# Layer 2's pass of a graph network: stored lookup one-hots loaded two batches at a time into four buffers

## What is computed

```
h = maximum(layernorm(x), 0)
message = h[src] * (edge_weight_n2 * edge_weight)[:, None]
x = x + segment_sum(message, dst, num_segments=6250)
```

## Time and profile before

| what | us |
|---|---|
| median of three runs | 7052.06 |
| the runs | 7048.93 to 7054.1 |
| span of the profiled execution | 7043.7 |
| layer 2's pass in it, first DMA issue to last accumulation (4152.3 to 4887.1) | 734.8 |

### The profile page before, as it was taken

The page is one execution under the profiler, slowest core; times in us unless marked ns, Lnnn a source line. Parts: engine busy times, 40 slices in busy tenths (PEclk is TensorE's granted clock), DMA queues, the critical chain, the costliest instruction groups (busy, mean ns, idle before and its releaser), DMA issues. The chain is left out here.

```text
span 7043.7 us, 136888 instructions
## 1 busy us (share of the span) xinstructions
PE 4278.3 (61%) x28588; PEld 2975.8 (42%) x28784; DVE 4223.4 (60%) x20793; ACT 3158.6 (45%) x10013; POOL 5145.6 (73%) x5914
## 2 busy tenths in 40 slices
PE   4433333333346666666666558998777777777774
PEld 3333333333343333332333237776455555555553
DVE  4333333333337666666666678888776666666666
ACT  1000000000014555555555558887466666666664
POOL 6777777777747777777777758886577777777774
PEclk6555555555556766677676779999887777777776
DMA  4333333333335666666666647775433333333331
GB/s 136 96 104 104 101 98 104 104 101 98 104 78 160 169 170 169 170 169 170 168 169 170 169 144 237 243 242 203 170 80 80 78 80 79 78 80 78 80 80 48
DMA packets 658227, 909.24 MB, mean 129 GB/s; under 512 B 141934, under 2 KB 424624, under 8 KB 657905
## 3 DMA queue, kind: packets, MB, share of 16 engines
q1 hardware_dynamic: 481126, 599.15, 27.0%
q0 software_dynamic: 175648, 308.58, 19.0%
q10 hardware_dynamic: 1357, 0.47, 0.0%
HBM read 697.55 MB, written 210.23 MB: 129 GB/s over the span
## 5 line engine op out<-in xcount | busy, mean ns | idle before, releaser
L726 POOL DMA_INDIRECT rows<-src_rows,idx_slots x1568 | 1500.2, 957 | 535.0 <-issue 477.1
L726 POOL DMA_INDIRECT rows<-node_rows,idx_slots x1568 | 1500.0, 957 | 505.5 <-issue 475.4
L726 POOL DMA_INDIRECT rows<-rel_rows,idx_slots x1568 | 1486.7, 948 | 511.2 <-issue 450.8
L1160 PE MATMUL bank<-onehot,ones 128*128 128x512 f32 x1568 | 1241.5, 886 | 135.8 <-ACT onehot L1169 129.1
L1169 ACT ACTIVATE onehot<-ident,fresh_slots 128x128 f32<-128x128 f32 x3136 | 989.3, 386 | 38.3 <-DVE fresh_slots L1296 33.6
L928 ACT ACTIVATE rows<-edge_in 128x128 f32<-128x128 f32 x392 | 120.4, 309 | 1806.4 <-PE bank L948 1800.3
L977 DVE TENSOR_TENSOR wide_room<-bank,wide_room 96x128 f32 x392 | 112.6, 287 | 1322.5 <-PE bank L948 1322.4
L1257 PE MATMUL bank<-w_e,edge_in 128*128 128x256 f32 x784 | 403.5, 610 | 754.2 <-DVE onehots L805 719.8
L948 PE MATMUL bank<-onehots,rows 128*96 128x128 f32 x1568 | 393.7, 432 | 591.3 <-issue 537.4
L948 PE MATMUL bank<-onehot,rows 128*96 128x128 f32 x1568 | 386.8, 428 | 598.4 <-issue 320.7
L1240 ACT ACTIVATE onehot<-onehots,exp_bias 128x512 bf16<-128x512 f32 x392 | 283.0, 722 | 946.9 <-DVE max_by_chunk L1338 895.9
(11 more groups left out here) (282 smaller groups left out, 9980.7 us busy)
## 6 DMA issues: line engine op xcount, KB each, us to landing
edge_in<-dst_line SPq DMA_DIRECT2D x392, 256.0 KB, 4.2
spill<-rows SPq DMA_DIRECT2D x392, 256.0 KB
rows<-spill SPq DMA_DIRECT2D x392, 256.0 KB, 3.1
hot_rows<-rows SPq DMA_DIRECT2D x98, 712.0 KB, 3.7
onehots<-hot_rows SPq DMA_DIRECT2D x98, 712.0 KB, 4.4
onehots<-src_low SPq DMA_DIRECT2D x98, 512.0 KB, 6.4
edge_in<-in_ea_l SPq DMA_DIRECT2D x98, 256.0 KB, 4.2
rows<-node_rows,idx_slots POOLq DMA_INDIRECT x1568
```

The lines of the kernel that those rows point to most:

```text
L726: pool.indirect_dma_start(out=to[:, b.slot(ROW_RING), g, :], out_offset=None, in_=table, in_offset=bass.IndirectOffsetOnAxis(ap=idx_slots[ ...
L1160: return pe.matmul(bank, ones[:, :], diag[:, b.slot(2), :, :].rearrange("p g e -> p (g e)"), start=start, stop=True)
```

## The change

The buffers keep their size and place (eight batches in all) and are cut into four of two batches instead of two of four. Each DMA loads two batches out of the stored group of four, so it takes half of each stored row (2848 of 5696 bytes). The wait ahead of it is for batch t - 7 to be picked, where t is a multiple of 2. The stage `reload` gets lag 2, so that SP's list runs: one-hots of batches t and t + 1, then the spilled rows of batch t - 2. PE and DVE wait on one of four semaphores instead of one of two.

```diff
+HOT_GROUP, HOT_RING = 2, 4
...
-            :, 0:2 * EDGE_GROUP * HOT].rearrange("p (s n e) -> p s n e", s=2, e=HOT)
+            :, 0:2 * EDGE_GROUP * HOT].rearrange("p (s n e) -> p s n e", s=HOT_RING, e=HOT)
...
-                    s_hot = [ph.sem(f"hot{n}") for n in range(2)]
+                    s_hot = [ph.sem(f"hot{n}") for n in range(HOT_RING)]
...
                     def hot_of(b):
-                        return hot_in[:, b.of_group(EDGE_GROUP).slot(2), b.slot(EDGE_GROUP), :]
+                        return hot_in[:, b.of_group(HOT_GROUP).slot(HOT_RING), b.slot(HOT_GROUP), :]
...
                         def hots(b):
-                            if b.slot(EDGE_GROUP) == 0:
-                                if not b.early(2 * EDGE_GROUP):
-                                    sp.wait_ge(s_picked, b.v - EDGE_GROUP)
-                                slot = b.of_group(EDGE_GROUP).slot(2)
+                            if b.slot(HOT_GROUP) == 0:
+                                ahead = HOT_GROUP * HOT_RING
+                                if not b.early(ahead):
+                                    sp.wait_ge(s_picked, b.v + (HOT_GROUP - ahead))
+                                slot = b.of_group(HOT_GROUP).slot(HOT_RING)
+                                at = b.slot(EDGE_GROUP) * HOT
                                 sp.dma_start(hot_in[:, slot, :, :].rearrange("p n e -> p (n e)"),
-                                             hot_rows[group_at(b), :, :].rearrange(
-                                                 "o p e -> (o p) e")).then_inc(s_hot[slot], 16)
+                                             hot_rows[group_at(b), :, at:at + HOT_GROUP * HOT]
+                                             .rearrange("o p e -> (o p) e"))\
+                                  .then_inc(s_hot[slot], 16)
...
-                        pipeline(sp, [(0, hots), (0, reload)])
+                        pipeline(sp, [(0, hots), (2, reload)])
...
-                            landed(pe, s_hot, b.of_group(EDGE_GROUP), 16)
+                            landed(pe, s_hot, b.of_group(HOT_GROUP), 16)
...
-                            landed(dve, s_hot, b.of_group(EDGE_GROUP), 16)
+                            landed(dve, s_hot, b.of_group(HOT_GROUP), 16)
```

## The result

The changed kernel takes 6976.95 us (median of four runs, 6973.56 to 6981.03), the kernel before 7050.5 (four runs, 7047.45 to 7054.1). The ratio is 0.9893, with a 95% interval of 0.988 to 0.9906: 1.1% faster. The forecast was 6992, with a range of 6979 to 7024.

A forecast was written before the change was run, and what follows sets the result against it. PE's own 1.66 us step was taken as the bound: 73.8 us lost, less 7.2 (loop entry), 2.6 (start) and 4 (closeness), so 60 us gained. Span 7043.7 to 6984, median 8.4 above: 6992 us, range 6979 to 7024.

The forecast's parts named there:

- What bounds it, and where the loss is: Layer 2's pass: PE bounds at 1.66 us a step; late one-hots at batches that are multiples of 4; 73.8 us lost.
- Order on SP: SP's list: lag 2 on the spilled rows' reload lets one-hots be asked for earlier, lead 7.2 us in place of 3.9.
- The rows moved past it: Spilled rows on SP: reload goes out at most 0.2 to 0.3 us later, lead about 5.5 us, cost nothing.
- Rival 1: Spilled rows for POOL become the late ones; 30 us come back, 7022 us; chance 0.11.
- More DMAs, bytes: SP and DMA engines: 98 more issues at 0.6 us each, unchanged bytes, share 82%; cost nothing on the path.
- Rival 3: DMA engines become the bound because half-length rows cost as much as whole ones; 22 us slower, 7074 us; chance 0.04.
- turning point: DMA engines: shorter rows set the step once a half row costs over 0.89 of a whole one.
- The sum: Layer 2's pass: 73.8 less 7.2 less 2.6 is 64.0 us, less 4 for closeness, so 60 us gained.
- the find at 4163.09 waits 2.6 us for them, which stays or shrinks to nothing: Start of the pass: wait for eight reloads and two one-hot groups asked for at once; 2.6 us counted as not gained.
- the loop entry's 7.2 us: PE's entry into its hardware loop: a stop and two slow finds, 7.2 us taken to stay.
- Such closeness costs something: I take 0.01 us a step, 4 us: PE's steps: DVE, ACT and POOL within 0.1 us behind PE cost 4 us, bounds 0 and 12 us.
- The range: Whole kernel's time: 6980 to 7008 us for the forecast itself, 6979 to 7024 with most of the spilled-row rival.

The follow-up runs named there:

- e5_late_lead: Changed kernel with spilled rows back at lag 0 and one-hots of t waiting for pick t - 3 instead of t - 7: 7032.27 us, ratio 0.9979.
- e8_later_lead: Changed kernel with spilled rows back at lag 0 and one-hots of t waiting for pick t - 2 instead of t - 7: 7239.17 us, ratio 1.0276.
- e1_size_only: Changed kernel with the lag of the spilled rows taken back to 0, half loads kept: 6981.1 us, ratio 0.9904.
- second profile: Changed kernel run once more, unchanged, to be profiled again: 6978.7 us, pass 665.4 us.
- e3_one_batch: Changed kernel with one-hots loaded one batch at a time into eight buffers, lag 2 kept: 6978.43 us, ratio 0.9902.
- second pair: Changed kernel and kernel before, each run once more unchanged for another profile: 6978.7 and 7049.31 us, passes 665.4 and 735.8 us.
- e4_two_parts: Changed kernel with the third bf16 part of the facts left out of find's matmuls: 6959.0 us, ratio 0.9875.
- e2_lag_only: Changed kernel with one-hots again loaded four batches at a time into two buffers, lag 2 kept: 6982.67 us, ratio 0.9905.

## Why the prediction was right in kind and wrong in size

**What bounds it, and where the loss is:** right. The finds at multiples of 4 were the lost time, and the cause was a lead of 3.9 us against landings of 3.9 to 5.8. `e5_late_lead` and `e8_later_lead` bring the waits back by the moment of asking alone, and they pay 0.28 us a load for a mean shortfall of 0.29, and 1.37 us for one of 1.37. One reading was incomplete: ACT's 1.56 us a batch left out `relu`. With it ACT is busy 97.3 of 100 us in the changed kernel, 1.61 us a batch, and stands 0.05 us below PE's step, not 0.1.

**Order on SP:** right, 7.5 us against 7.2 forecast. But the text let the lag do the work and named the half size only in passing. `e1_size_only` shows that the size alone would have been enough, which the earlier trace rows (256 KB in 3.1 us) beside the earlier trace rows could have told.

**The rows moved past it:** cost nothing, as taken. Their longest landing even fell from 5.6 to 4.1 us (4.2 in the second profile). Rival 1 is out: after the pass's first one POOL had no wait for spilled rows.

**More DMAs, bytes:** nothing on the path, as taken. The issue price of 0.6 us was 0.47 by `e3_one_batch`. The share rose to 85% where 82% and a bound of 100% were given. Loads overlapped as the trace of before had shown. The Trainium skill, DMA: Bandwidth & Descriptors, Anatomy of one DMA, would have a half load there in 2.8 us (the estimate made ahead), and it took 3.4 in the median beside the other traffic. The rule of the Trainium skill, DMA: Bandwidth & Descriptors, Bandwidth, to batch to 1 MiB and more, is about the share of the peak rate, and it decided nothing here: with the DMA engines 80 to 88% busy, loads of 178 KB (6978.43 us) did as well as those of 712 (6982.67). Rival 3 had rows of half length cost as much as whole ones. With 41% of the bytes in them that would have taken the share from 80 to over 110%; it went to 85. Its turning point was worked out wrongly: 0.55 x (2 x 0.95 - 1) = 0.49, so a half row would have had to cost 0.95 of a whole one, not 0.89, for the step to be as long as before. The estimate from the runs is 0.58.

**The sum is the step that failed,** in two terms. In the two pairs of profiles the pass shrank by 73.2 and 70.4 us; the sum had 60.

- *"the find at 4163.09 waits 2.6 us for them, which stays or shrinks to nothing"*: the sum took the 2.6 off the 73.8 us as if it stayed, though the first steps hold no `sums` and are short enough to make up for it. The first six steps took 10.08 us, 6 x 1.66 = 9.96: next to nothing of the loss was there. Without the start and the loop entry's 7.2 us the loss was 722.9 - 10.1 - 7.2 - 385 x 1.66 = 66.5 us, and 66.2 of it went. That is 2.2 us over the 64.0 of the sum.
- *"Such closeness costs something: I take 0.01 us a step, 4 us"* (up to 12 in the range) was nothing. From 4181.77 to 4806.24 PE did 376 steps in 624.5 us, 1.661 each.

Smaller: the first load landed 1.2 and 1.1 us earlier, which stood in the range but not in the sum, and the stop at the loop entry was 1.2 and 1.0 us shorter, which was not foreseen. These four terms make 60 + 2.2 + 4 + 1.2 + 1.2 = 68.6 for the first pair. The other 4.6 us are the missing fall of the clock at the loop entry (2 x 1.35) and a faster start (8.20 us for the first six steps in place of 10.08). Neither is there in the second pair: the clock falls in both of its profiles, and the first six steps take 9.42 us in place of 9.28. They are chance of the execution. The second pair had more to lose, 69.0 us outside the start and the loop entry, and 68.7 of it went; with the first load's 1.1 and the stop's 1.0, less 0.4 for the start and the clock, that is its 70.4.

**The range** ended at 6979. Its low end gave back the 2.6, the 4 and the first load's 1, and a few stray us, so the two mis-sized terms alone would not have led out of it. It left no room for the shorter stop, for the clock and the start, which differ from one execution to the next, or for the baseline, whose median was 7052 when I forecast and 7044.7 to 7050.5 in later runs. Of the 15 us between the forecast and the median, 13.2 are the pass's, and 3.1 come from adding 8.4 us from span to median, which are 5.3 here; 1.2 go the other way, since outside the pass this profile is that much longer.

## What to carry to other kernels

When a pipelined load is late by a little, work out its lead (from the issue to the first use, in undisturbed steps of the bounding engine) beside the row of landings: the difference is paid in full for each load, where, as here, the next load is asked for only after work that waited for this one. Once the lead is longer the whole loss goes at once. Shortening the load and asking earlier are two ways to the same end; either was enough. And where one engine's own step is longer than every other's, even by 0.05 us as here, take the new time as that step times the count, with nothing for closeness.

## What was not expected of the hardware

- PE stops for 2.7 to 3.5 us on entering its hardware loop in five of the kernels with loads of 356 KB or less, and for 4.4 to 4.5 us in the two with loads of 712 KB. `e4_two_parts`, with loads of 356 KB and fewer matmuls, has no such stop. The cause is open.
- How long a load takes to land did not follow the mean traffic. A load of 356 KB took 3.4 us in the median at 268 GB/s and 3.0 at 187, but the spilled rows beside it took 3.1 and 3.3, and a load of 712 KB took 4.4 at 241 GB/s and 4.2 at 267 (`e2_lag_only`). What is in flight beside a load seems to matter: at the same 267 to 268 GB/s the spilled rows took 3.6 us in the median and 5.3 at the longest beside one-hot loads of 712 KB (`e2_lag_only`), and 3.1 and 4.1 beside those of 356 KB. Which part of this is the size and which the order of asking was not separated.
